# Rounding the tail's weights with casting DMAs and spreading a group's weight preparation over all its slots, in a cross-attention and feed-forward kernel

## The reference, cut to what matters

```python
q  = _ln(fp8_linear(ln_out, wq));  qx = _ln(fp8_linear(ln_out, wqx))
k  = _ln(fp8_linear(ln_out, wk));  v  = fp8_linear(ln_out, wv)
kx, vx = split(einsum(cond, w_kv_x))          # kx goes through _ln too
core, xout = gqa(q, k, v), gqa(qx, kx, vx)
catq = div_clamp_fp8(concatenate([core, xout]), proj_smooth)
x1 = x + einsum(catq, wproj) * (proj_in_scale * proj_w_scale)
# feed-forward: the int32 weights stand for (wq - 128) * scale
out = x1 + qlinear(silu(qlinear(z, gate)) * qlinear(z, up), down)
```

## Time and profile before

| | us |
|---|---|
| median of three runs | 1794.38 |
| lowest, highest | 1790.72, 1794.49 |
| the profiled execution | 1790.16 |
| its span in the trace | 1788.4 |
| PE busy in the span | 1652.6 (92%) |
| ACT, DVE, POOL busy | 1396.7 (78%), 1365.1 (76%), 1137.6 (64%) |

### The profile page before, as it was taken

How to read it: one execution, slowest core, us unless ns; L and a number is a source line. 1 busy time by engine, 2 the same in 40 slices (tenths; PEclk the granted TensorE clock), 3 DMA queues, 4 the chain that set the end, 5 groups by cost and what they waited for, 6 DMA issues and landing times.

```text
span 1788.4 us, 43867 instructions
## 1 busy us (share of the span) xinstructions
PE 1652.6 (92%) x15491; PEld 1229.4 (69%) x15776; DVE 1365.1 (76%) x3182; ACT 1396.7 (78%) x2944; POOL 1137.6 (64%) x1043
## 2 busy tenths in 40 slices
PE   1449999999999999999999999999999889999999
PEld 1337778878887887788788877877788544444444
DVE  8969888997998799889979987998777652323232
ACT  6888999999999999999999999999999713121211
POOL 1127788778878877887787788778877613020212
PEclk9669999999999999999999999999999999999999
DMA  5566789888988988888887978888999971212100
GB/s 183 171 197 125 145 158 169 144 148 164 152 159 142 171 156 140 160 169 144 155 162 154 152 144 180 152 148 163 175 202 199 197 213 59 74 68 102 39 23 24
DMA packets 675894, 258.51 MB, mean 145 GB/s; under 512 B 620513, under 2 KB 639201, under 8 KB 675681
## 3 DMA queue, kind: packets, MB, share of 16 engines
q1 hardware_dynamic: 675680, 255.76, 71.0%
HBM read 75.15 MB, written 29.51 MB: 59 GB/s over the span
## 4 chain that ended last, share of the span: by engine, by line
ACT 27%; PE 21%; DVE 20%; POOL 14%; issue 11%; SPq 4%; DMA 3%; ACTq 0%; DVEq 0%; POOLq 0%
POOL local L1159 10%; ACT local L1071 7%; ACT local L1068 7%; ACT local L991 5%; DVE w_raw L1229 4%; PE ps_s L743 4%; ACT local L978 3%; DVE local L1401 3%; POOL w_raw L1143 2%; DVE sq_sum L1314 2%; PE ps_pj L868 2%; PE ps_s L882 2%; PE ps_o L868 2%; SPq L628 2%; PE ps_pj L869 2%
## 5 line engine op out<-in xcount | busy, mean ns | idle before, releaser
L1159 POOL TENSOR_TENSOR local<-local 128x512 bf16<-128x512 f32 x512 | 592.9, 1158 | 258.3 <-ACT local L1071 257.9
L736 PE MATMUL ps_pj<-wide 128*128 128x256 bf16 (+1 forms) x5544 | 584.6, 255 | 6.5 <-DVE wide L1238 4.0
L736 PEld LDWEIGHTS ps_pj<-wide 128*128 128x128 bf16 x5544 | 469.2, 98 | 116.5 <-ACT local L991 7.1
L1068 ACT ACTIVATE local<-ps_s,neg_max 128x512 f32<-128x512 f32 x512 | 379.4, 741 | 34.2 <-DVE neg_max L1393 30.6
L783 PE MATMUL ps_o<-v_hi,local 128*128 128x129 bf16 x2048 | 375.8, 221 | 8.0 <-DMA local<-local 4.9
L1071 ACT ACTIVATE local<-ps_s,neg_max 128x512 bf16<-128x512 f32 x512 | 381.2, 745 | 0.0
L785 PE MATMUL ps_o<-v_hi,local 128*128 128x129 bf16 x2048 | 375.2, 219 | 0.0
L784 PE MATMUL ps_o<-local 128*128 128x128 bf16 x2048 | 375.1, 218 | 0.0
L1393 DVE TENSOR_REDUCE neg_max<-ps_s 128x1 f32<-128x512 f32 x512 | 344.7, 673 | 36.9 <-PE ps_s L803 36.1
L991 ACT ACTIVATE local<-ps_pj,head_rstd 128x128 f32<-128x128 f32 x756 | 233.3, 414 | 52.3 <-issue 51.4
L1129 POOL TENSOR_TENSOR head_rstd<-sq_sum,minus_half 128x3 f32<-128x3 f32 x256 | 240.5, 939 | 27.8 <-DVE sq_sum L1314 27.8
(11 more groups left out here) (122 smaller groups left out, 2666.0 us busy)
## 6 DMA issues: line engine op xcount, KB each, us to landing
quantised_heads<-local SPq DMA_DIRECT2D x128, 128.0 KB, 2.5
w_raw<-w_group SPq DMA_DIRECT2D x56, 256.0 KB, 3.2
wide<-quantised_heads SPq DMA_DIRECT2D x3, 4096.0 KB, 13.3
local<-local SPq DMA_TRANSPOSE x640, 3.2
wide<-packed_weights SPq DMA_DIRECT2D x32, 256.0 KB, 3.1
wide<-x SPq DMA_DIRECT2D x7, 1024.0 KB, 8.6
w_raw<-w_proj SPq DMA_DIRECT2D x10, 512.0 KB, 4.6
wide<-quantised_heads SPq DMA_DIRECT2D x16, 256.0 KB, 3.4
```

The lines of the kernel that those rows point to most:

```text
L736: last = mm(dst[:, at:at + n], lhs, w_at(par, part, c, cross * 512 + at, n), start=(k == 0), stop=(k == len(terms) - 1))
L1068: a(p_exp[:, u % 2], ps_s[u % 2][:], ACT.Exp, bias=neg_max[:, u % 4:u % 4 + 1])
L1159: tt_(pp[:, u % PP_BUFS, 1], p_exp[:, u % 2], pp[:, u % PP_BUFS, 0], ALU.subtract)\
```

## The change

The kernel after does four things.

1. The packing through SBUF is gone: `pre_load`, `pre_store`, `pack` on ACT, `pack_load`, `pack_store` and `pack` on POOL, with SP's waits for them. In its place POOL issues nine DMAs from DRAM to DRAM that convert on the way, four of 128x4096 fp32 and five of up to 128x3380 int32, right after the third layer norm's power in the opening. The host lays the inputs out so that each partition's part of a row is contiguous. POOL's scratch for DMA descriptors stays at 1024 bytes a partition, as L1563 has it.
2. The offset of -128 is taken off after the tail's loads: DVE does 11 in-place instructions of 128x1024 bf16 in group 7 (slots 30 to 45) and 6 after the first batch's `z_rest`, before `hidden(0, 1)`. PE waits for DVE's count where it waited for the loads.
3. From group 2's weights on, each chunk has the same place in a quarter: counted within the quarter's 16 slots, sums at 15 of the quarter before, then scale steps of 1, 3, 1 and 2 heads at slots 2, 3, 6 and 7, the high part in two halves at 8 and 9, the low part at 11. Chunk 0 is prepared in the last quarter of the group before. Group 1's weights keep their old slots.
4. Loads of the chunks move with them, and the first two chunks of group 1 are loaded in the opening instead of one.

```diff
-        OPENING_PIECES = [*range(WP_PIECES), PIECES - 1]
-        GROUP_PIECES = [*range(WP_PIECES, PIECES - 1)]
-        PER_GROUP = 3
-        PACK = ((39, 43, 47, 0), (49, 51, 55, 0), (53, 59, 63, 1))
...
-        SCALE_CUTS = (0, 3, 7)
-        PREP = {"sums": (2, 10, 22, 31), "scale0": (6, 14, 26, 38), "scale1": (7, 15, 27, 39),
-                "hi": (9, 17, 32, 41), "lo": (11, 19, 35, 43)}
-        EARLY_LOADS, HALF_STEP = 1, 2
-        LOADS = (58, 2, 16, 24)
+        SCALE_CUTS = (0, 1, 4, 5, 7)
+        FIRST_PREP = {"sums": (2, 10, 22, 31), "scale0": (6, 14, 26, 38), "scale1": (6, 14, 26, 38),
+                      "scale2": (7, 15, 27, 39), "scale3": (7, 15, 27, 39), "hi0": (9, 17, 32, 41),
+                      "hi1": (9, 17, 32, 41), "lo": (11, 19, 35, 43)}
+        PREP = {"sums": 3, "scale0": 6, "scale1": 7, "scale2": 10, "scale3": 11, "hi0": 12, "hi1": 13, "lo": 15}
+        PREP_BASE = (-20, -4, 12, 28)
+        EARLY_LOADS, HALF_STEP = 2, 2
+        LOAD_BASE = (-32, -16, 0, 16)
+        FIRST_LOADS = {CH + 2: 16, CH + 3: 24, 2 * CH: 40}
...
+        def prep_at(g, slot, step):
+
+            at = SLOTS * g + slot
+            found = [CH + c for c in range(CH) if at == FIRST_PREP[step][c]]
+            return found + [CH * t + c for t in range(2, G) for c in range(CH)
+                            if at == SLOTS * (t - 1) + PREP_BASE[c] + PREP[step]]
...
-            for i in range(len(OPENING_PIECES)):
-                pre_store(i)
-                if 3 <= i + 2 < len(OPENING_PIECES):
-                    pre_load(i + 2)
-                if i == 4:
-                    load_ctx(3)
-            for i in range(len(OPENING_PIECES) - 3, len(OPENING_PIECES)):
-                sp.wait_ge(pre_out[i % 3], 16 * (i // 3 + 1))
-
+            for b in range(1, B):
+                load_ctx(b)
...
                 if n == 0:
-                    sp.wait_ge(pack_out[0], 16 * 2 * (G - 1))
-                    sp.wait_ge(pack_out[1], 16 * (G - 1))
+                    for landed in cast_out:
+                        sp.wait_ge(landed, 16)
...
-                for n in range(max(2 * i - 1, 0), 2 * i + 1):
-                    pack(n)
             head_norm(TILES - 1, TILES - 1, 0)
             ctx_part(2)
-            for n in range(2 * TILES - 1, len(OPENING_PIECES)):
-                pack(n)
...
+            def cast(n):
+                if n < WP_CASTS:
+                    cols_of = slice(WP_CUT * n, WP_CUT * (n + 1))
+                    src, dst = w_proj[:, cols_of], packed[:, cols_of]
+                else:
+                    at = FFN_CUT * (n - WP_CASTS)
+                    end = min(at + FFN_CUT, CH * 2 * HID + HC * DM)
+                    src, dst = w_ffn[:, at:end], packed[:, GU_AT + at:GU_AT + end]
+                nc.gpsimd.dma_start(dst, src).then_inc(cast_out[n], 16)
...
                 tt_(shift[:], neg_mean[:], rstd[:], ALU.mult).then_inc(ln_rstd, 1)
+                if b == 2:
+                    for n in range(WP_CASTS + FFN_CASTS):
+                        cast(n)
...
+            def take_offset(n):
+                for landed, count in tail_waits(n + 1):
+                    dve.wait_ge(landed, count)
+                view = tail_piece(n)[1]
+                v.tensor_scalar(view, view, -ZERO_POINT, None, ALU.add).then_inc(offset_done, 1)
```

More of the change, by code:

```diff
@@ L46 @@
 FP8_MAX = 448.0
+ZERO_POINT = 128.0
 EXPONENT = 0x7F80
@@ L398, in turn_at, with load_at @@
             return [(q, j) for j, (q, rest) in enumerate(at) if rest == 0 and q < n and (q >= 0 or not first)]
-        def prep_at(slot, step, last):
-            return [c for c in range(CH) if PREP[step][c] == slot and not last]
+        def prep_at(g, slot, step):
[3 more added lines that the diff above has]
+                            if at == SLOTS * (t - 1) + PREP_BASE[c] + PREP[step]]
+        def load_at(n):
+            return FIRST_LOADS.get(n, SLOTS * (n // CH - 1) + LOAD_BASE[n % CH])
         def tile_place(k):
@@ L925, in weight_scale, with weight_hi @@
                 last.then_inc(w_scaled, 1)
-            def weight_hi(par, c, count):
+            def weight_hi(par, c, count, half=None):
                 act.wait_ge(w_scaled, count)
                 act.sem_inc(waited_act, 1)
-                a(w_par(par, c * GW, GW), raw(c), ACT.Copy).then_inc(w_hi_done, 1)
+                at, end = (half * GW // 2, (half + 1) * GW // 2) if half is not None else (0, GW)
+                done = a(w_par(par, c * GW + at, end - at), raw(c)[:, at:end], ACT.Copy)
+                if half != 0:
+                    done.then_inc(w_hi_done, 1)
             act.wait_ge(scales_ready, 1)
@@ L1059, in group @@
                         qk_whole(q, j, GROUP_TURNS * g + 3 * (2 + q) + j)
-                    for c in prep_at(slot, "hi", last):
-                        if first and c == 0:
-                            act.wait_ge(ctx_lo_done, ctx_pieces(2))
-                        weight_hi((g + 1) % 2, c, CH * g + CH + c + 1)
+                    for half in range(2):
+                        for n in prep_at(g, slot, f"hi{half}"):
+                            if n == CH and half == 0:
+                                act.wait_ge(ctx_lo_done, ctx_pieces(2))
+                            weight_hi(n // CH % 2, n % CH, n + 1, half)
                     for u in unit_at(slot, EXP_LAG, first):
@@ L1162, in group @@
                         head_power(tile_place(k)[1], GROUP_TILES * g + TILES + k)
-                    for j, (_, pack_slot, _, _) in enumerate(PACK if not last else ()):
-                        if slot == pack_slot:
-                            pack(g, j)
             for g in range(G):
@@ L1407, in group @@
                             ctx_piece(CTX_DIRECT + n // CH, n % CH)
[L1408 to L1409 removed]
+                    for n in prep_at(g, slot, "sums"):
+                        weight_sums(n % CH, n + 1)
                     if last and CLIP_FIRST <= slot < CLIP_FIRST + HEADS_PIECES:
@@ L1502, in _ @@
                 z_rest(0, tt)
+            for n in range(X_DONE, X_DONE + WD_PIECES):
+                take_offset(n)
             dve.wait_ge(sdown_in, 16)
```

133 lines of the change are left out of this document (27 added, 106 removed).

## The result

The changed kernel took 1769.75 us (median of 4 runs, 1766.94 to 1771.61), the kernel before 1793.14 (4 runs on the same chip, 1790.72 to 1794.49): a ratio of 0.9865, 95% interval [0.9846, 0.9883], 23.4 us less. The forecast was 1756, in a range of 1746 to 1794. The profiled execution took 1770.42 us (span 1768.6), 19.7 less than that of before.

A forecast was written before the change was run, and what follows sets the result against it. PE bounds the main loop; DVE, then ACT, the opening. Gains of 14.2 (opening), 21.4 (groups 1 to 6) and 0.8 (group 0), 36.4 us, take the profiled 1790.2 to 1753.8; forecast for the median 1756, range 1746 to 1794.

The forecast's parts named there:

- The opening: Before the first score: ACT loses 17 copies and waits for loads, so the first score moves from 130.1 to 115.9, 14.2 us.
- The casts: Nine converting DMAs issued by POOL in the opening: cost taken as 0, ending at 109 us, before the first DMA transpose.
- the cover: POOL's idle time in the opening, about 20 us after layer norm 2's power, claimed to hide nine issues of up to 2.2 us.
- Rival 1: Opening: POOL held at its DMAs by the small descriptor scratch; 1774 or 1817 us; chance 0.20 still faster, 0.14 slower.
- the 51 + 13 us of the working: Opening: 51 us for the casts' 17.0 MB read at 332 GB/s, 13 more for 4.2 MB of contexts and chunks.
- Rival 2: Casts still running beside group 0's DMA transposes cost 5 to 39 us, giving 1761 to 1795; chance 0.12.
- The rule that the prediction took from the Trainium skill: Opening: GpSimd's DMA descriptors can't be written while DVE runs an operation taking both ports, so issues come late.
- The main loop: Groups 1 to 6: evenly spread chunks bring quarters from 40.84 to 39.95 us, 0.25 above PE's need, saving 21.4 us.
- its lower bound of 8: Groups 1 to 6: smallest gain expected, 8 us, with quarters of 40.5 as quarter 3 has without any preparation.
- rival 3: Groups 1 to 6: a chunk in every quarter leaves none to catch up in; quarters 40.5, gain 8 us, 1770; chance 0.08.
- the 27.4 of the bound: Groups 1 to 6: largest gain expected, 27.4 us, with every quarter at the 39.7 us that PE needs.
- Group 0, group 7, the tail: Group 0's last quarter gains 0.8 us; eleven subtractions in group 7 (5.2 us on DVE) and the tail's six cost 0.

The follow-up runs named there:

- the run with old slots: The changed kernel with only the casts kept: every group's chunks have the slots and loads of the kernel before; 1777.45 us, ratio 0.9911.

## Why the forecast was right, and where it was not

The sign and the range held; the forecast was 14 us too low. On the profiled executions the sum was 16.6 too good (1753.8 for 1770.4), and one term made 13.6 of that.

**The opening: right, 13.3 for 14.2.** The working gave tile 7's evacuation at 105.4 and its `head_norm` at 107.2; the timelines of DVE and ACT have

```profile
106.24 0.54 DVE L1233 TENSOR_REDUCE sq_sum<-local 128x3 f32<-128x387 f32 x1
```

```profile
108.27 0.88 ACT L917 ACTIVATE local<-ps_s,head_rstd 128x128 f32<-128x128 f32 x3 [0.84 <-POOL head_rstd L1058]
```

so both came 1 us late and the first score with them (116.8 for 115.9). The row that answers to the first of the earlier trace rows:

```profile
83.22:106.24 23.02, 11.76 (x73) 9.12 (x71) 22.81 (x21) 19.40 (x41) 6.78 (x6) 0.72 0.67 189
```

DVE is busy 22.81 of 23.02 us, so its order set this stretch, as the prediction said. The wait and the copies behind `head_norm` gave the other 3.4.

**The casts: right at 0, by the cover it named.** Rival 1's mechanism is there, but weaker: it priced a hold until six of the nine had landed, and here seven could be outstanding, so two landings were enough. The last issue was over at 58.8 us and the cover ended at 64.8. The bytes went faster than the 51 + 13 us of the working: 17.0 MB read in 48.8 us, 349 GB/s, from 44.7 to 93.5, and of the 4.2 MB beside them only two contexts, 2.1 MB, came in that time. Rival 2 did not happen, since no cast was left at 116 us. The rule that the prediction took from the Trainium skill, "SBUF — State Buffer", section "SBUF: two separate sides", would have the issues wait for some of DVE's operations. The trace agrees where it can tell: the first seven stood beside DVE's TENSOR_TENSOR and TENSOR_REDUCE and took 0.5 us each (0.7 the first), and the one at 52.87, beside a TENSOR_SCALAR of 128x4096 bf16 that ended at 53.99, took 1.25 and was over at 54.12. With twice as many casts two took 1.22 and 1.46 and also ended 0.1 us after such an operation. The price is 0.7 to 0.9 us an issue; the holds of 4 us are not of this kind, since they are gone with the larger scratch. The Trainium skill says in "DMA: Bandwidth & Descriptors", section "SWDGE vs HWDGE vs iDMA", that these descriptors stand in rings in SBUF; seven casts at 1024 bytes and at least nine at 2048 agree with that.

**The main loop: this step failed.** It was "24 x (40.84 - 39.95) = 21.4", and in it "0.25 because half of `weight_hi` now stands in slot 8". The 0.25 measured 0.8, and the term 7.8, just under its lower bound of 8. Two things make the 0.8.

The first half of the rounding in slot 8, in front of that slot's exponentials, costs 0.53. I took half of a 0.5 us instruction as hidden; nothing hides it there. Quarter 0 before, from which I took 39.7, had its whole rounding at slot 9.

The other 0.3 is backlog from the quarter ahead, which the sum put at nothing. It is there in group 6's last quarter, without a chunk, and with both halves at 9 in every quarter (40.01), while the first quarter with both halves at 9 behind a quarter without preparation is at 39.73 (groups 2 to 6 of the run with old slots). That is rival 3's mechanism, no quarter to catch up in, with 0.3 of its 0.8. The prediction's argument against it, that "quarter 0 follows a quarter with packings and is at PE's floor all the same", didn't hold: a packing is POOL's work, a chunk is ACT's and DVE's. So the time came out at rival 3's number (quarters of 40.5, 1770) by its mechanism in the smaller part.

Neither is bound to the even spread. With roundings at 9 and 12, each in a gap of ACT's, no backlog is left to hand on: every quarter can carry a chunk and most are at 39.7, 39.80 on average, with a loop of 955.1 us, 25.0 less than before, near the 27.4 of the bound.

**Group 0, group 7, the tail.** Group 0 gained nothing for the 0.8. The eleven subtractions of group 7 were put at 0, because DVE is busy 123 of 162 us there; they cost 0.7 to 2.6 us. They also took 0.41 to 1.36 us each, 10.6 in all, for the 5.2 of the prediction; the six of the tail took 0.42 each or less. A share of busy time doesn't tell whether a slot has room. The six cost nothing that shows: the tail's 352.1 us are within 0.3 of before.

## What to carry to other kernels

When side work is spread over a pipelined loop, find the engine whose gaps are rarest in the slots concerned, measure each gap and each step, and give each step a gap of its own, behind the slot's critical instruction and not ahead of it. Cutting a step smaller helps only if the pieces go into different gaps: here quarters with the same two halves stand 0.8 us above PE's floor at slots 8 and 9, 0.3 with both at 9, and 0.1 at 9 and 12. Before you take the time of one stretch as what every stretch can reach, ask what the stretch ahead of it left behind: the best quarter here followed one that had no preparation. Casting DMAs cost GpSimd some 5 us of issuing here and delayed nothing, since it had idle time, but count how many can be outstanding, and keep what the engine must do next behind a cover longer than the hold.

## What the runs showed of the hardware that was not expected

- With 1024 bytes of descriptor scratch, seven casts could be outstanding, for casts of 0.95 MB written and for casts of half that; with 2048 bytes all nine went out at once. A cast was 144 packets in either size. GpSimd went on 0.3 us after a cast had landed.
- An issue of a cast kept GpSimd 0.51 us, and 1.22 to 1.46 beside a TENSOR_SCALAR of 128x4096 bf16 on VectorE; while it was held, the profile names no releaser, only "issue".
- Nine casts from fp32 to bf16 read 17.0 MB in 48.8 us (349 GB/s), and a context load of 1 MB beside them took 25.1 us, from 50.49; the same load took 5.1 in the kernel before.
- The same offset subtraction (128x1024 bf16, in place, VectorE) took 0.41 to 1.36 us in group 7 and 0.42 in the tail.
